# The last tile's matrix products of each MLP stage moved into the next step, and the next image's normalisation one tile pair behind instead of two

## The reference

```python
h = layer_norm(x, n1_g, n1_b)
h = afno_filter(h, w1, b1, w2, b2)   # rfft2, a two-stage 16x16 block MLP per frequency, softshrink, irfft2, + h
h = h + x
residual = h
h = layer_norm(h, n2_g, n2_b)
h = gelu(h @ mw1 + mb1)              # 128 -> 512
h = h @ mw2 + mb2                    # 512 -> 128
out = h + residual
```

## Time and profile before

| | |
|---|---|
| median of 3 runs | 1695.14 us (1693.17 to 1696.4) |
| profiled execution | 1697.64 us |
| its span, first to last instruction | 1695.9 us |
| granted TensorE clock, mean | 0.996 |
| share of the chain that ended last | PE 88%, DVE 4%, POOL 2%, ACT 2% |

### The profile page before, as it was taken

One profiled execution on the slowest core, in us unless ns is written; L12 is line 12 of the kernel. 1 busy time (PEld: TensorE's weight loads), 2 busy tenths in 40 slices (PEclk: granted clock), 3 DMA queues, 4 the chain that ended last, 5 costly groups with the idle time before them and its releaser, 6 DMA issues.

```text
span 1695.9 us, 35295 instructions
## 1 busy us (share of the span) xinstructions
PE 1611.5 (95%) x11336; PEld 1458.9 (86%) x11336; DVE 1136.1 (67%) x2879; ACT 949.7 (56%) x1774; POOL 628.3 (37%) x792
## 2 busy tenths in 40 slices
PE   0799999999999999999999999999999999999999
PEld 0799978888999988888889998888889998788888
DVE  7979576666649856666666976666664795665563
ACT  3655366666535546666634644666663563666665
POOL 3900037776710005777760000777774000111111
PEclk9999999999999999999999999999999999999999
DMA  8400613333300062333320024333332006011111
GB/s 215 180 26 1 227 43 99 105 99 105 101 32 1 13 226 77 110 93 103 108 88 1 1 94 138 94 100 111 105 101 69 2 1 207 14 38 31 37 31 50
DMA packets 166369, 138.86 MB, mean 82 GB/s; under 512 B 9218, under 2 KB 129284, under 8 KB 166276
## 3 DMA queue, kind: packets, MB, share of 16 engines
q1 hardware_dynamic: 165988, 137.15, 25.4%
q10 hardware_dynamic: 288, 0.46, 0.1%
HBM read 70.47 MB, written 67.11 MB: 81 GB/s over the span
## 4 chain that ended last, share of the span: by engine, by line
PE 88%; DVE 4%; POOL 2%; ACT 2%; issue 1%; DMA 0%; DVEq 0%; ACTq 0%
PE ps L692 27%; PE ps L683 7%; PE ps L685 7%; PE ps L639 7%; PE ps L684 7%; PE ps L578 7%; PE ps L534 6%; PE ps L524 5%; PE ps L549 3%; PE ps L672 3%; PE ps L551 3%; PE ps L658 3%; PE ps L664 3%; POOL first L1273 1%; POOL xout L1269 1%; DVE stats L943 1%
## 5 line engine op out<-in xcount | busy, mean ns | idle before, releaser
L692 PEld LDWEIGHTS ps<-mw,gel 128*128 128x128 f32 x4096 | 533.2, 191 | 43.3
L692 PE MATMUL ps<-mw,gel 128*128 128x128 f32 x4096 | 536.4, 274 | 0.0
L803 ACT ACTIVATE gel<-ps,mb1f 128x512 f32<-128x512 f32 x512 | 351.7, 687 | 266.6 <-PE ps L685 235.6
L1314 POOL TENSOR_TENSOR arena<-arena,mb2rep 128x512 f32<-128x512 f32 x128 | 163.8, 1281 | 796.4 <-ACT hn L789 796.4
L683 PE MATMUL ps<-hth,mw1h 128*128 128x512 f32 x512 | 259.9, 508 | 7.5 <-DVE htl L1111 6.5
L1307 POOL TENSOR_SCALAR arena<-xnext,rstd,shift 128x128 f32<-128x128 f32 x384 | 168.8, 463 | 219.4 <-DVE shift L1238 219.4
L789 ACT ACTIVATE hn<-arena,shift,rstd 128x128 f32 (+1 forms) x512 | 221.5, 482 | 24.2 <-DVE shift L1238 23.9
L1094 DVE TENSOR_TENSOR arena<-ps,arena 128x512 f32 (+1 forms) x60 | 41.4, 691 | 259.6 <-PE ps L664 240.9
L685 PE MATMUL ps<-hth,mw1l 128*128 128x512 f32 x512 | 202.1, 395 | 0.0
L684 PE MATMUL ps<-htl,mw1h 128*128 128x512 f32 x512 | 200.9, 392 | 0.0
L774 ACT ACTIVATE osb<-usb,vectors 128x512 f32<-128x512 f32 (+1 forms) x136 | 95.7, 704 | 121.1 <-DVE usb L1002 121.1
(11 more groups left out here) (101 smaller groups left out, 2434.8 us busy)
## 6 DMA issues: line engine op xcount, KB each, us to landing
arena<-aside SPq DMA_DIRECT2D x128, 256.0 KB, 4.8
aside<-gz SPq DMA_DIRECT2D x96, 256.0 KB, 2.9
between<-xout SPq DMA_DIRECT2D x62, 256.0 KB, 2.3
xnext<-between SPq DMA_DIRECT2D x62, 256.0 KB, 3.0
out_dram<-xout SPq DMA_DIRECT2D x62, 256.0 KB, 2.3
aside<-first SPq DMA_DIRECT2D x32, 256.0 KB, 2.3
xnext<-in_x_dram SPq DMA_DIRECT2D x31, 256.0 KB, 3.0
mw1raw<-in_L_mw_dram SPq DMA_DIRECT2D x4, 256.0 KB, 2.5
```

What stands on the lines that cost most here:

```text
L692: mm = pe.matmul(ps[:, r % 2, P * i:P * i + P], gel[:, r % 2, m, P * i:P * i + P], mw2[:, m, :], start=(m == 0 and i == 0), stop=(m == CHU ...
L803: act.activation(gel[:, r % 2, m, :], ps[:, 2 + m % 2], ACT.Gelu, bias=mb1f[:, m:m + 1]).then_inc(gelu_out, 1)
L1314: pool.tensor_tensor(t, t, b, ALU.add).then_inc(mb2_done, 1)
```

## The change

Tile 31 (`HELD`) of steps 0 to 2 no longer gets its products in its own `mlp` stage. Its transposed halves stay in SBUF, its residual with the bias is put into a new tile `hold`, and the weights of both layers get places of their own, so that they are loaded and split once a layer instead of once a step. In the next step `fc1_held(0)` and `(1)` come ahead of the filter's last `mix2`, `fc1_held(2)` and `(3)` around `first_pair`, and `fc2_held` in place of `keep_warm(14)`; ACT's `gelu_held` and DVE's `held_out` go with them, and SP stores the tile in that step. The last step keeps its tile, as before.

The next image is normalised one pair behind: pair q takes the xnext pair q - 1 from pair 4 on; pairs 2 and 3 take the xnext pairs 0 and 1 as before, and a new `nearer()` with a third place in `stats`, `rstd` and `shift` takes xnext pair 2 between pair 3 and pair 4. The chain of pair 17 and `last_tile` go in steps 0 to 2. POOL biases tile t in the turn of xnext tile t, no longer tile t + 2, and the biases of tiles 0 and 1 are no longer ahead. `lower(1)` and `hi(1)` come earlier, the transpose of tile 1 stands behind the first product group.

```diff
+NEAR = 3
...
+HELD = TILES - 1
+HELD_BANK = (6, 7, 0, 2)
...
+        hold = at("hold", [P, ROWS, C], o); o += size(hold.shape)
...
-                        sp.wait_ge(x_st[i], 16 * (TILES // 2) * s)
-                    sp.wait_ge(row0_st, 16 * s)
+                        sp.wait_ge(x_st[i], 16 * (TILES // 2 * s - i))
+                    sp.wait_ge(row0_st, 16 * (s - 1))
                     for r in range(4):
                         sp.wait_ge(gz_st[r], 16 * (TILES // 4) * s)
                 else:
                     sp.wait_ge(early_st, 16 * EARLY)
                     sp.wait_ge(late_st, 16 * (TILES - EARLY))
-                load_raw(layer)
+                if s % IMAGES == 0:
...
+                if s:
+                    sp.wait_ge(x_out, X_CREDIT + TILES * s)
+                    transfers(sp, target[s - 1], xout[:, HELD % 2], HELD // 4, HELD % 4, x_st[HELD % 2], row0_st, True)
...
-                pe.wait_ge(x_out, X_CREDIT + TILES * s)
+                pe.wait_ge(x_out, X_CREDIT + TILES * s - (s > 0))
...
+                    elif s:
+                        fc1_held(s, 0)
+                        fc1_held(s, 1)
...
+            def fc1_held(s, m):
+
+                if m == 0:
+                    pe.wait_ge(lo_out, TILES * s)
+                    pe.wait_ge(y_done, (UNITS + 1) * s + 7)
+                products((s - 1) // IMAGES, HELD, m, ps[:, HELD_BANK[m]])
+
+            def fc2_held(s):
+
+                for m in range(CHUNKS):
+                    pe.wait_ge(gelu_out, CHUNKS * (TILES * s - 1) + m + 1)
+                    for i in range(ROWS):
+                        mm = pe.matmul(ps[:, HELD % 2, P * i:P * i + P], gel[:, HELD % 2, m, P * i:P * i + P],
+                                       mw2[:, (s - 1) // IMAGES, m, :], start=(m == 0 and i == 0), stop=(m == CHUNKS - 1),
+                                       skip_group_check=True)
+                mm.then_inc(f2_mm, 1)
...
                 turned(s, SOON + 3)
+                if s:
+                    turned(s, CGROUPS - 4)
+                    fc1_held(s, 2)
                 first_pair(s, SOON, CGROUPS)
-                mlp_bias(s)
+                if s:
+                    fc1_held(s, 3)
+                if s % IMAGES == 0:
+                    mlp_bias(s)
                 idft_w(s, 1)
-                keep_warm(14)
+                if s:
+                    fc2_held(s)
+                else:
+                    keep_warm(14)
                 turn(s, 0, 0)
                 keep_warm(5)
-                pe.wait_ge(mlp_w, s + 1)
+                pe.wait_ge(mlp_w, s // IMAGES + 1)
+                pe.wait_ge(mlp_b, s // IMAGES + 1)
                 for m in range(CHUNKS):
                     fc1(s, 0, 0, m)
-                    if m == 1:
-                        pe.wait_ge(mlp_b, s + 1)
+                    if m == 0:
                         turn(s, 1, 1)
-                pe.wait_ge(mlp_in, MLP_IN * (s + 1))
+                pe.wait_ge(mlp_in, MLP_IN * (s // IMAGES + 1))
...
+                end = TILES if s == len(STEPS) - 1 else HELD
 
                 def tile(j, r):
                     n = 4 * j + r
                     known = n if isinstance(j, int) else 4
                     for m in range(CHUNKS):
-                        if known + 1 < TILES:
+                        if known + 1 < end:
...
+                    late = s < len(STEPS) - 1 and (not isinstance(j, int) or n // 2 > NEAR)
+                    act.wait_ge(rs_done, RS * s + 2 * j + r // 2 + 1 + late)
...
+            def gelu_held(s, m):
+                act.wait_ge(f1_mm, CHUNKS * (TILES * s - 1) + m + 1)
+                if m == 0:
+                    act.wait_ge(f2_mm, TILES * s - 2)
+                act.activation(gel[:, HELD % 2, m, :], ps[:, HELD_BANK[m]], ACT.Gelu,
+                               bias=mb1f[:, (s - 1) // IMAGES, m:m + 1]).then_inc(gelu_out, 1)
...
+                    gelu_held(s, 0)
+                    gelu_held(s, 1)
...
+                    gelu_held(s, 2)
+                    gelu_held(s, 3)
...
-                    if m == 2:
+                    if m == 1:
                         hi(s, 1, 1)
...
+            def held_out(s):
+
+                dve.wait_ge(f2_mm, TILES * s)
+                dve.wait_ge(mlp_w, s // IMAGES + 1)
+                dve.wait_ge(x_st[HELD % 2], 16 * (TILES // 2 * s - 1))
+                dve.tensor_tensor(xout[:, HELD % 2].rearrange("p h c -> p (h c)"), ps[:, HELD % 2],
+                                  hold[:, :, :].rearrange("p h c -> p (h c)"), ALU.add).then_inc(x_out, 1)
...
+                    nxt = not last and LAG <= known <= PAIRS
+                    near = known > NEAR
...
-                    if nxt and known >= 4:
-
-                        dve.wait_ge(z_new, TILES * s + 2 * q - 6)
+                    if nxt and near:
+
+                        dve.wait_ge(z_new, TILES * s + 2 * q - 4)
                     if nxt:
                         for e in range(2):
-
-                            dve.wait_ge(xn_in[2 * h + e], 16 * (TILES // 4 * s + i))
-                            if isinstance(i, int) and 2 * (q - LAG) + e == TILES - 1:
+                            r = 2 * (1 - h if near else h) + e
+                            dve.wait_ge(xn_in[r], 16 * (TILES // 4 * s + i + (h if near else 0)))
+                            if isinstance(i, int) and 2 * (q - 1) + e == TILES - 1:
                                 dve.wait_ge(row0_in, 16 * (s + 2))
                             rows_ = slice((2 + e) * ROWS, (3 + e) * ROWS)
-                            ins = bn(xnext[:, 2 * h + e], 0, stats[:, h, rows_, :])
+                            ins = bn(xnext[:, r], 0, stats[:, h, rows_, :])
+                    if known == 1:
+                        lower(s, 1, 1)
...
-                    if 1 <= known <= PAIRS:
+                    if 1 < known <= PAIRS:
...
+                def nearer():
+
+                    for e in range(2):
+                        dve.wait_ge(xn_in[e], 16 * (TILES // 4 * s + 2))
+                        ins = bn(xnext[:, e], 0, stats[:, 2, (2 + e) * ROWS:(3 + e) * ROWS, :])
+                    own.add(ins)
+                    own.settle()
+                    a, b = 2 * ROWS, 4 * ROWS
+                    inverse_std(dve, own, stats[:, 2, a:b, 2], var[:, a:b], rstd[:, 2, a:b], nt0[:, a:b])
+                    dve.scalar_tensor_tensor(shift[:, 2, a:b], stats[:, 2, a:b, 1], -1.0, rstd[:, 2, a:b],
+                                             ALU.mult, ALU.mult).then_inc(rs_done, 1)
+
                 pair(0, 0)
-                shift_bias(s)
+                if s % IMAGES == 0:
+                    shift_bias(s)
                 pair(0, 1)
+                if s:
+                    held_out(s)
                 dve.wait_ge(resid_in[1], RESID_IN[1] * (s + 1))
                 pair(1, 0)
                 pair(1, 1)
+                if not last:
+                    nearer()
...
-                for n in range(TILES):
-                    j, r = n // 4 - 1, n % 4
-                    if j >= 0 and not last:
-                        ready(j, r)
-                        z_rows(j, r)
-                        scaled(j, r)
-                    if n >= 2:
-                        biased(n - 2)
-                    if j >= 0 and not last:
-                        added(j, r)
+                if last:
+                    for n in range(TILES):
+                        biased(n)
+                    continue
                 j = TILES // 4 - 1
-                if not last:
-                    ready(j, 0)
-                    z_rows(j, 0)
-                    z_rows(j, 1)
-                for n in (TILES - 2, TILES - 1):
+                for n in range(TILES - 4):
+                    ready(n // 4, n % 4)
+                    z_rows(n // 4, n % 4)
+                    scaled(n // 4, n % 4)
                     biased(n)
-                if not last:
-                    ready(j, 2)
-                    z_rows(j, 2)
-                    z_rows(j, 3)
-                    scaled(j, 0)
-                    for r in range(4):
-                        if r < 3:
-                            scaled(j, r + 1)
-                        added(j, r)
+                    added(n // 4, n % 4)
+                for r in (0, 2):
+                    ready(j, r)
+                    z_rows(j, r)
+                    z_rows(j, r + 1)
+                    biased(4 * j + r)
+                    biased(4 * j + r + 1)
+                scaled(j, 0)
+                for r in range(4):
+                    if r < 3:
+                        scaled(j, r + 1)
+                    added(j, r)
...
+                    p = 2 * j + r // 2
+                    h = p % 2 if p < 2 else 2 if p == 2 else (p + 1) % 2
...
+                    if 4 * j + r == HELD and not last:
+                        pool.wait_ge(x_out, X_CREDIT + TILES * s)
+                        pool.tensor_tensor(hold[:, :, :], t, b, ALU.add).then_inc(mb2_done, 1)
```

(16 more changed lines are left out.)

85 lines of the change are left out of this document (46 added, 39 removed).

## The result

The changed kernel is slower: 1717.3 us median (1715.7 to 1724.74, 4 runs) beside 1694.16 us (1690.81 to 1696.4, 4 runs) on the same chip, a ratio of 1.0145 with a 95% interval of 1.0123 to 1.0168. 1723 was forecast. The execution that was profiled took 1724.74 us, with a span of 1723.0, 27.1 us more than the span before; +27.8 was forecast for it.

The account below looks back on a forecast made before the run. TensorE (PE), busy 95% of the span, was taken as the bound. Terms: -18.0 + 0.5 - 3.6 + 10.4 + 23.4 + 5.1 + 7.6 + 2.4 = +27.8 us, on the median 1723 us; range 1688 to 1742.

Parts of the forecast that it names:

- End of the stage: End of an MLP stage, three times: tile 31's products and second matmuls go, net -6.0 us each, -18.0.
- Where the work goes: Held tile's work in the next step: nearly all covered by PE's gaps and replaced filler matmuls, +0.5 us in all.
- Head: Start of the stage: earlier `lower(1)` brings tile 1's first product about 1.2 us forward in steps 1 to 3, -3.6.
- (a): First pairs, steps 0 to 2: fc2 of tile 2 waits for `x_new(0)` behind POOL's bias, 1.4 us a step.
- (b): First pairs, steps 0 to 2: fc2 of tile 4 waits for `x_new(2)` behind POOL's bias, 2.0 us a step.
- (c): Pair 4, steps 0 to 2: `nearer()`'s small operations wait for POOL, `lower(6)` is late, PE idles 3.15 us a step.
- (d): Pair 4, steps 0 to 2: tile 7's load behind a store and its chain behind POOL delay `lower(7)`, 4.65 us a step.
- Clock: After the long stall of (d), PE's granted clock dips: 5.1 us in three steps, bounds 0 and 10.
- Every later pair: Eleven pairs in three steps: the load issued behind a store lengthens each by 0.23 us, 7.6 us in all.
- Start of step 2: DVE's first weight part waits longer for POOL's tail to end, and PE with it: +2.4 us.
- faster: Rival: loads land in time, bunching is absorbed, only bias waits stay, 1684 us; without these too, 1674; chance 0.18.
- Port free: Rival: DVE's small operations slip between POOL's, so (c) costs nothing and (d) 0.95 us; 1695 us, chance 0.12.

Follow-up runs that it names:

- held_only: The changed kernel with its held tile, but the next image two tile pairs behind and POOL's order as before the change: 1690.35 us.
- no_held_tile: `one_behind_load_ahead` without the held tile, the last tile being finished in its own step: 1689.41 us.
- halves: `load_ahead` with each two-input instruction of POOL made as two of half the size: 1712.88 us.
- one_behind_load_ahead: The changed kernel with the next image one pair behind from the second pair on and SP's load ahead of the store: 1672.35 us, measured again 1673.85.
- load_ahead: The changed kernel with SP issuing the next image's load ahead of the store of an earlier result, instead of behind it: 1703.61 us.
- build_later: `one_behind_load_ahead` with the second layer's spectral weights built three evictions later on DVE: 1671.24 us.
- bias_head: `load_ahead` with POOL's biases of tiles 0 to 3 only moved two tiles ahead of the z rows: 1673.28 us.
- bias_ahead: The changed kernel with all of POOL's biases two tiles ahead of the z rows, as before the change: 1735.15 us.
- quiet_chain: `bias_head` with POOL kept off tiles 2 and 3 until DVE's `nearer()` is done: 1696.26 us.

## Why the prediction was right

The forecast was 1723 for 1717.3 us, and +27.8 for +27.1 us of span. The mechanism is the one forecast, wait by wait, except for how DVE passes POOL (below). But part of the agreement is luck. The two sums agree more closely than their terms, and the execution that gives +27.1 is the longest of four, with 5.0 us of lower clock in two filters that nobody forecast; by the medians the change costs 23.1 us. Of the signs named, one did not come: no small operation of DVE took over 2 us in the first pairs (1.24 at most).

- **End of the stage.** -18.0 forecast, -17.7 measured. `held_only` confirms what the prediction checked first: the DFT waits for the last z rows, and only the nearer schedule takes them out of the way. `x_new(28)` held fc2(30) 0.21 and 0.31 us where 0.4 was taken.
- **Where the work goes.** +0.5 forecast, nothing measured: from the DFT to the first product of step 1 it is 163.65 us before and after, and `no_held_tile` shows the same. PE's wait at `mix2` fell from 7.9 to 3.8 us in the kernel, and that for the column evictions from 3.1 to 0.8.
- **Head.** -3.6 forecast, -4.6 measured: 1.48 in steps 1 and 2, 1.44 in step 3 and 0.21 in step 0, where nothing was taken.
- **(a) and (b).** 10.4 forecast (its own 1.4 and 2.0 give 10.2); the waits are 1.36 to 1.38 and 1.77 to 1.87 us, 9.5 in all, and the six pairs are 11.0 longer. The granted clock is 1.00 in them (240 to 262, 655 to 677), so the 0.25 us that each pair loses beyond its wait is not clock; the profile doesn't say what it is. Plain waits in order on one queue are the easiest to price.
- **(c) and (d).** 23.4 forecast as waits, and 5.1 of clock behind them: 28.5. The three pairs are 24.3 us longer, so 4.2 less; this is the term that was mis-sized. The waits in them are 2.68 to 2.75 and 3.47, 1.65 and 1.90, 15.2 us in all. They should not be set against the 23.4 alone, since a slower PE comes later to its next wait and waits less there: in step 1 the low clock (0.62 from 688 to 692, after 2.75 us of idle) lies between (c) and (d). The step that was wrong is the one that let no small operation past until POOL's run was over. One passes for each of POOL's instructions, which `halves` shows by changing only their size. The alternative in the sentences on the Trainium skill ("SBUF — State Buffer", "SBUF: two separate sides": the lock is held for one instruction) is what the chain's rows show. By that rule the sum would have been 24.2, and its 3.6 us are most of the 4.2. The rows do not bear it out everywhere: the 8.15 us at 889.57 are again the length of six to seven of POOL's instructions. The rows of before could hardly have told: the small operations that were held met one instruction of POOL's each (0.83 to 1.28 us), except the one of 2.63 us in each step.
- **Clock.** Within these three pairs 9.1 us go beyond the waits. The windows account for up to 8.4 of them: the granted clock is 0.72 over 280 to 292, 0.62 and 0.96 over 688 to 692 and 692 to 696, and 0.83 and 0.76 over 1111 to 1121 and 1121 to 1128. A further 5.0 us stand in the filters of steps 0 and 3, with windows at 0.91 (175 to 195) and 0.83 (1340 to 1360); before, the two stretches were 2.0 and 3.0 us shorter. Nothing forecast these, and they filled what (c) and (d) left. No row ties them to the change: the wait of 1.39 us just ahead of the dip in step 0 stands in both traces (at 179.82 and 179.17), with a dip behind it only in one, and two executions of one kernel differ in the same way (`one_behind_load_ahead`).
- **Every later pair.** 7.6 forecast, 7.2 measured (0.9 of it in the last pair of step 1), and `load_ahead` shows that the cause is the one given.
- **Start of step 2.** +2.4 forecast, +2.1 measured; `build_later` shows the place.

Of the rivals, "faster" said that without the bias waits and without the bunching behind them the change would come to 1674. That is what it came to (1673 and 1672), but only after the order of POOL's biases or of the image's pairs, and the order of SP's loads, were mended. "Port free" fell: the chain does wait for POOL.

## What to carry to other kernels

Before work is moved one slot nearer to its use, list every queue that serves it in order: here the compute half of the move was sound and worth 6.35 us a boundary, and nearly all of the loss was gone once a load was no longer issued behind a store, nor a bias queued behind other work. When several waits follow one another on the same queues, mend the first and measure again, since the later ones may only be its echo (`bias_head`: 9 us expected, 30 gained). An instruction that waits in an engine's queue also holds back everything that stands behind it there and what that frees for others: `bias_ahead` and `quiet_chain` paid 18 and 23 us for that.

## What the runs showed of the hardware

Small DVE operations of 0.17 us took 1.15 to 1.28 us beside POOL's two-input instructions of 1.28, and 0.58 to 0.66 beside those of 0.71: each waited for the end of one instruction, those with one input (L325, L327) too. Beside POOL's z rows, one-input instructions of 0.46 us, they took 0.17 to 0.4 us; the two of 0.40 in step 1 (678.14 and 678.57) each end 0.02 to 0.03 us after a z-row instruction, so this may be the same waiting on a smaller scale. DVE's 128x512 operation with an input in PSUM at 697.12, next to POOL's z rows, and that at 676.07, beside a two-input instruction of POOL's, took 0.69 us, as elsewhere. In the tail of a step, where POOL's instructions follow one another in the same way, single DVE operations waited over two of them (2.63 us) or over six to seven (8.15 us). What decides between the two cases is open; no run here was made for it.
